# Transitions of a two-layer cross-attention kernel reordered: first loads and K/V, end of the attention, seam to layer 1

## The reference

```python
# layer 0: 32 query heads of 32, 8 key/value heads (4 query heads share one)
q = x @ Wq + bq;  k = ctx @ Wk + bk;  v = ctx @ Wv + bv
attn = softmax(q k^T / sqrt(32) + mask)            # over 64 keys
x = layer_norm(attn v @ Wo + bo + x) * gamma + beta
# layer 1: 16 heads of 64, no biases
a = layer_norm(ctx) * ln_gamma + ln_beta
Q = x @ Wq1.T;  K = a @ Wk1.T;  V = a @ Wv1.T
attn = softmax(where(mask, Q K^T / 8, -inf))
out = x + tanh(gate) * (attn V @ Wo1.T)
```

## Time and profile before

| | |
|---|---|
| median of three runs | 1812.03 us (1809.41 to 1812.71) |
| profiled execution, its own time | 1808.57 us |
| its span | 1806.8 us |
| PE busy | 1737.9 us, 96% |
| DVE, ACT, POOL busy | 60%, 32%, 61% |
| mean granted clock of TensorE | 0.99 |
| DMA | 278 MB, 154 GB/s |

### The profile page before, as it was taken

One profiled execution on the slowest core, in us unless ns is written; L12 is line 12 of the kernel. 1 busy time (PEld: TensorE's weight loads), 2 busy tenths in 40 slices (PEclk: granted clock), 3 DMA queues, 4 the chain that ended last, 5 costly groups with the idle time before them and its releaser, 6 DMA issues.

```text
span 1806.8 us, 22550 instructions
## 1 busy us (share of the span) xinstructions
PE 1737.9 (96%) x8576; PEld 1445.9 (80%) x8576; DVE 1090.4 (60%) x1070; ACT 582.8 (32%) x666; POOL 1104.6 (61%) x610
## 2 busy tenths in 40 slices
PE   5999999999999899999999988899999999999998
PEld 4788888888888688888888867788888888888887
DVE  6888888888879444444444453646644664466442
ACT  3444444444445433333333322213311331133110
POOL 3577777777789856565655585536543664466431
PEclk9999999999999899999999989899999999999999
DMA  9433332332326556666667844454845474556332
GB/s 215 107 80 76 85 79 73 88 80 72 75 80 175 171 184 236 207 240 212 233 227 233 291 138 141 140 171 132 256 130 173 130 224 147 163 161 189 124 121 94
DMA packets 273515, 278.02 MB, mean 154 GB/s; under 512 B 64512, under 2 KB 224384, under 8 KB 273408
## 3 DMA queue, kind: packets, MB, share of 16 engines
q1 hardware_dynamic: 272256, 275.53, 49.3%
q10 hardware_dynamic: 1152, 1.05, 0.3%
HBM read 174.77 MB, written 101.71 MB: 153 GB/s over the span
## 4 chain that ended last, share of the span: by engine, by line
PE 64%; DVE 16%; issue 8%; ACT 5%; POOL 3%; DMA 2%; SPq 1%; DVEq 0%; ACTq 0%
PE ps L53 20%; PE ps L55 20%; PE ps L54 20%; DVE small L1023 4%; DVE pr L1046 4%; ACT pr L795 3%; DVE pT0r L1057 2%; DVE pT1r L1057 2%; DVE xT0r L953 2%; ACT ot L789 2%; DVE xT1r L953 2%; PE ps L657 1%; PE ps L665 1%; PE ps L632 1%; POOL oc1l L1276 1%
## 5 line engine op out<-in xcount | busy, mean ns | idle before, releaser
L1324 POOL TENSOR_TENSOR x2Tl<-x2r,x2Th 128x1024 fp32r<-128x1024 f32 x32 | 76.9, 2403 | 292.1 <-ACT x2Th L896 292.1
L1130 DVE STREAM_TRANSPOSE x2r<-xd 128x1024 f32<-128x1024 f32 x32 | 68.7, 2147 | 207.9 <-PE ps L55 207.9
L1264 POOL TENSOR_TENSOR pr<-pr,small 128x1024 f32<-128x1024 f32 x64 | 121.9, 1905 | 99.8 <-DVE small L1052 99.8
L896 ACT CAST x2Th<-x2r 128x1024 fp32r<-128x1024 f32 x32 | 33.7, 1052 | 375.9 <-DVE x2r L1130 375.9
L1259 POOL TENSOR_TENSOR pr<-pr,small 128x1024 f32<-128x1024 f32 x64 | 123.9, 1936 | 20.9 <-DVE small L1027 20.9
L1023 DVE TENSOR_REDUCE small<-pr 128x16 f32<-128x1024 f32 x64 | 78.1, 1220 | 78.2 <-ACT pr L795 78.2
L1281 POOL TENSOR_TENSOR xb<-xb,bo 128x1024 f32<-128x1024 f32 x32 | 78.6, 2455 | 73.6 <-DMA xb<-in_x_dram 73.6
L1295 POOL TENSOR_TENSOR y<-y,bet 128x1024 f32<-128x1024 f32 x32 | 76.8, 2399 | 74.8 <-DVE y L1069 74.8
L1100 DVE TENSOR_TENSOR y<-ps,xb 128x512 f32<-128x512 f32 x64 | 44.0, 688 | 114.1 <-PE ps L55 111.2
L53 PE MATMUL ps<-wo0h,oc0l 128*128 128x512 f32 x256 | 104.4, 408 | 5.5 <-DVE wo0l L977 3.0
L53 PE MATMUL ps<-wo0h,oc1l 128*128 128x512 f32 x256 | 103.1, 403 | 5.7 <-DVE y L1100 5.7
(11 more groups left out here) (368 smaller groups left out, 5503.3 us busy)
## 6 DMA issues: line engine op xcount, KB each, us to landing
o_scratch<-ot SPq DMA_DIRECT2D x256, 64.0 KB, 1.8
ocr<-o_scratch SPq DMA_DIRECT2D x16, 1024.0 KB, 7.4
xb<-in_x_dram SPq DMA_DIRECT2D x32, 512.0 KB, 6.7
x_scratch<-y SPq DMA_DIRECT2D x32, 512.0 KB, 5.2
a_scratch<-ost SPq DMA_DIRECT2D x64, 256.0 KB, 3.5
b_scratch<-ost SPq DMA_DIRECT2D x64, 256.0 KB, 5.0
xd<-x_scratch SPq DMA_DIRECT2D x128, 128.0 KB, 2.9
raw<-b_scratch SPq DMA_DIRECT2D x64, 256.0 KB, 5.9
```

Of the source, the lines that this page charges most:

```text
L1264: nc.gpsimd.tensor_tensor(heads(v), heads(v), mx.unsqueeze(2).to_broadcast([P, TPB * GRP, KEYS]), ALU.subtract)\
L1324: nc.gpsimd.tensor_tensor(x2T[1][:], x2r[:], f32(x2T[0][:]), ALU.subtract).then_inc(x2_lo, 1)
```

## The change

The order of steps is changed at the three transitions, and a few waits and places in memory with it.

- **First loads and K/V.** Wk is requested by ACT ahead of x0 and x1, no longer by SP behind ctx. The biases of q and k come as rows, by three short loads right behind ctx, and PE turns them into columns, for which it waits ahead of ctx's turn; ACT copies them out. DVE makes wk0l before ctxTl, then turns all four x tiles; V's low half goes to POOL; DVE makes the low halves of x tiles 2 and 3, POOL those of 0 and 1. V is computed in PSUM banks of its own and needn't wait for K's evacuation. SP loads K for units 0 and 1 when K's stores are done, then stores V, loads the third piece of Wq, and only then V of units 0 and 1. The loads of gamma1 and beta1 move into slot 11.
- **End of the attention.** Chunk 0 of the output product is loaded in slot 16 and split in quarters in slots 20, 24, 28 and 32, no longer in slots 58 to 62. Wo's groups 5 and 6 are split in slot 63, group 7 in slot 64 ahead of DVE's turn. The statistics of the context's norm come after the queries' low half; its coefficients come behind the first residual; its rows are scaled on ACT in slot 65; chunk 1's low halves are made in slot h = 2.
- **Seam to layer 1.** From chunk 2 on `coefficients` stands between the two halves of `chunk_lo`. The A pieces are loaded two in each of four slots, and DVE makes six of the low halves (0, 1, 2, 4, 5, 7), POOL two (3, 6). The first probabilities have their own place `pd0`, are summed and scaled ahead of the slot's output work, and are loaded right behind their store; B's pieces 2 and 4 to 7 are requested after they are turned. `prob_hi`, `prob_lo` and `turn_prob` of unit 0 move ahead of the B pieces.
- **Last outputs.** PE waits for each half of O by itself, and the last tile is stored in two halves.

```diff
+        pd0 = at("pd0", 140, [P, TPB, D // TPB])
...
+        def a0_low(h):
+            i = h - (LEAD + TAB * KT + 2)
+            return ((0,), (1, 2), (4,), (5,), (7,))[i] if 0 <= i < 5 else ()
...
-            return (6, 7) if u == UNITS else (u - (UNITS - 6),) if UNITS - 6 <= u < UNITS else ()
+            return (7,) if u == UNITS else (5, 6) if u == UNITS - 1 else (u - (UNITS - 6),) if UNITS - 6 <= u < UNITS else ()
+
+        def chunk0(u):
+            i, r = divmod(u - 2 * KT - 4, 4)
+            return i if 0 <= i < 4 and r == 0 else None
...
-            sp.dma_start(wkr[:], w["Wk0"].rearrange("(k p) n -> p k n", p=P)).then_inc(kv_ld0, 16)
+            sp.dma_start(brow[:KT], w["bq0"].rearrange("(g p) -> g p", p=P)).then_inc(b_ld, 16)
+            sp.dma_start(brow[KT:], w["bk0"].rearrange("(h p) -> h p", p=P)).then_inc(b_ld, 16)
+            sp.dma_start(bv_row[:], row(w["bv0"], KV0)).then_inc(b_ld, 16)
...
-            for u in range(2):
-                load_k(u)
-                load_v(u)
...
+            sp.wait_ge(zeroed, 4)
+            sp.wait_ge(kv_st, 16 * 8)
+            load_k(0)
+            load_k(1)
+            store_v()
             load_wq(2)
+            sp.wait_ge(vv_st, 16 * 4)
+            load_v(0)
+            load_v(1)
             load_wq(3)
...
+                if u == KT + 3:
+                    load_norm()
+                if u == 2 * KT:
+                    load_chunk(0)
...
-                    sp.wait_ge(x_turned, NTILE)
-                    load_chunk(0)
...
-                    sp.dma_start(pd[32 * a:32 * (a + 1)], d["p"][u % 2, :, 256 * a:256 * (a + 1)]
+                    sp.dma_start((pd if u else pd0)[32 * a:32 * (a + 1)], d["p"][u % 2, :, 256 * a:256 * (a + 1)]
...
-                    for c in range(4):
-                        load_a0(c)
-                if h == LEAD + TAB * KT + 1:
-                    for c in range(4, KT):
+                if 0 <= (i := h - (LEAD + TAB * KT)) < 4:
...
                     sp.wait_ge(o_done, SLOTS - 4)
-                    for c in range(3):
+                    for c in range(2):
                         load_raw(1, 0, c)
                 if h == SLOTS - 2:
                     load_xd(2)
                 if h == SLOTS - 1:
                     turn_prob(0)
+                    load_pd(0)
 
...
                     sp.wait_ge(o_done, SLOTS)
-                    for c in range(3, KT):
+                    load_raw(1, 0, 3)
+                    sp.wait_ge(p1_turned, 1)
+                    for c in (2, 4, 5, 6, 7):
                         load_raw(1, 0, c)
-                    load_pd(0)
                     for v in range(2):
                         load_xt(v)
...
+            pe.wait_ge(b_ld, 48)
+            nc.tensor.transpose(PJ[0][:, :KT + 2], brow[:], ident[:KT + 2, :KT + 2]).then_inc(b_turned, 1)
...
-                pe.wait_ge(kfull, r + 1)
                 for k in range(KT):
-                    last = three(nc, V[r][:, :KV0], [ctxT[x][:, k, P * r:P * (r + 1)] for x in (0, 1)],
+                    last = three(nc, PJ[r], [ctxT[x][:, k, P * r:P * (r + 1)] for x in (0, 1)],
...
-                after(pe, out_done, 2 * u)
                 for c in range(KT):
                     n, q = divmod(c, 4)
+                    if q == 0:
+                        after(pe, out_done, 2 * u - 1 + n)
...
+            act.dma_start(wkr[:], w["Wk0"].rearrange("(k p) n -> p k n", p=P)).then_inc(kv_ld0, 16)
             load_x(act, 0)
             load_x(act, 1)
+            act.wait_ge(b_turned, 1)
+            nc.scalar.copy(small[:, :KT + 2], PJ[0][:, :KT + 2]).then_inc(b_done, 1)
+            act.wait_ge(kv_ld0, 16)
+            nc.scalar.copy(wk[0][:], wkr[:]).then_inc(kv_hi, 1)
             act.wait_ge(ctx_t, 1)
             for i in range(4):
                 nc.scalar.copy(ctxT[0][:, 2 * i:2 * i + 2, :], C2[:, HALF * i:HALF * (i + 1)]).then_inc(ctx_hi, 1)
-            act.wait_ge(kv_ld0, 16)
-            nc.scalar.copy(wk[0][:], wkr[:]).then_inc(kv_hi, 1)
-            split_x(0)
-            split_x(1)
             act.wait_ge(kv_ld1, 16)
             nc.scalar.copy(wv[0][:], wvr[:]).then_inc(kv_hi, 1)
-            split_x(2)
+            for n in range(4):
+                split_x(n)
+            split_wq(0)
...
-                if UNITS - 6 <= u < UNITS - 2:
-                    chunk_hi(0, u - (UNITS - 6), 2)
-                if u == UNITS:
-                    for g in wo_groups(u):
-                        split_wo(g)
+                if (i := chunk0(u)) is not None:
+                    chunk_hi(0, i, 2)
+                if u == UNITS + 1:
                     norm_rows(0)
                     norm_rows(1)
...
                     split_x2(v + 1)
-                    exponential(v)
+                if v == 0:
+                    exponential(0)
                 slot(u)
                 if u >= UNITS:
                     out_slot(u - UNITS)
                     prepare(u - UNITS)
+            for c in range(2):
+                split_ab(1, 0, c)
+            exponential(1)
             affine(NTILE - 1)
-            for c in range(5):
-                split_ab(1, 0, c)
             prob_hi(0)
-            for c in range(5, KT):
+            for c in range(2, KT):
                 split_ab(1, 0, c)
             for u in range(2, NTILE):
...
+            dve.wait_ge(kv_hi, 1)
+            nc.vector.tensor_tensor(wk[1][:], wkr[:], f32(wk[0][:]), ALU.subtract).then_inc(kv_lo, 1)
             for i in range(4):
                 split_ctx(ctxT, i, i + 1)
-            turn_x(0)
-            turn_x(1)
-            dve.wait_ge(kv_hi, 1)
-            nc.vector.tensor_tensor(wk[1][:], wkr[:], f32(wk[0][:]), ALU.subtract).then_inc(kv_lo, 1)
-            turn_x(2)
-            turn_x(3)
-            dve.wait_ge(kv_hi, 2)
-            nc.vector.tensor_tensor(wv[1][:], wvr[:], f32(wv[0][:]), ALU.subtract).then_inc(kv_lo, 1)
-            dve.wait_ge(b_ld, 48)
+            for n in range(4):
+                turn_x(n)
+            dve.wait_ge(b_done, 1)
             for h in range(2):
                 dve.wait_ge(k_done, h + 1)
                 nc.vector.tensor_scalar(kf[:, h], V[h][:, :CTX], bk[:, h:h + 1], SCALE0, ALU.add, ALU.mult).then_inc(kfull, 1)
+            split_x(2)
+            split_x(3)
+            split_wq(0)
...
-                if u in (UNITS - 2, UNITS - 1):
-                    norm_stats(2 * (u - (UNITS - 2)))
-                    norm_stats(2 * (u - (UNITS - 2)) + 1)
...
+                if u == UNITS:
+                    split_wo(7)
...
-                if u == 0:
-                    dve.wait_ge(y_done, SLOTS)
...
-                if 0 <= (i := h - (LEAD + TAB * KT + 2)) < 4:
-                    low(0, 0, 2 * i + 1)
+                for c in a0_low(h):
+                    low(0, 0, c)
...
                     mask_max(v)
+                if v == 0:
+                    total(0)
                 slot(u)
                 if u >= UNITS:
                     out_slot(u - UNITS)
                     prepare(u - UNITS)
-                if v >= 0:
-                    total(v)
+            turn_prob(0)
+            total(1)
             gamma(NTILE - 1)
-            turn_prob(0)
             for c in range(1, KT, 2):
                 low(1, 0, c)
...
-            for n in range(4):
+            pool.wait_ge(kv_hi, 2)
+            pool.wait_ge(kv_lo, 1)
+            nc.gpsimd.tensor_tensor(wv[1][:], wvr[:], f32(wv[0][:]), ALU.subtract).then_inc(kv_lo, 1)
+            for n in range(2):
...
-                if UNITS - 5 <= u < UNITS - 1:
-                    chunk_lo(0, u - (UNITS - 5), 2)
-                if u == UNITS:
-                    norm_coefficients()
+                if (i := chunk0(u)) is not None:
+                    chunk_lo(0, i, 2)
...
                     residual(0)
+                    norm_coefficients()
                 if half == 1 and n + 1 < NTILE:
                     residual(n + 1)
+                if h == 2:
+                    for i in range(2):
+                        chunk_lo(1, i)
...
-                if h % 4 == 1 and h // 4 + 1 < NCHUNK:
-                    for i in range(2):
-                        chunk_lo(h // 4 + 1, i)
+                later = h % 4 == 1 and 1 < h // 4 + 1 < NCHUNK
+                if later:
+                    chunk_lo(h // 4 + 1, 0)
                 if half == 1:
                     coefficients(n)
+                if later:
+                    chunk_lo(h // 4 + 1, 1)
...
-                if 0 <= (i := h - (LEAD + TAB * KT + 2)) < 4:
-                    low(0, 0, 2 * i)
+                if h == LEAD + TAB * KT + 3:
+                    low(0, 0, 3)
+                if h == LEAD + TAB * KT + 6:
+                    low(0, 0, 6)
...
                     center(v)
+                if v == 0:
+                    scale(0)
                 slot(u)
                 if u >= UNITS:
                     out_slot(u - UNITS)
                     prepare(u - UNITS)
```

(9 more changed lines are left out.)

84 lines of the change are left out of this document (47 added, 37 removed).

## The result

| | before | changed |
|---|---|---|
| median of 5 runs | 1810.8 us | 1801.9 us |
| lowest to highest | 1809.4 to 1812.7 | 1800.3 to 1803.7 |
| ratio, 95% interval | 1 | 0.9953 (0.9942 to 0.9964) |
| profiled execution, its span | 1808.6, 1806.8 | 1800.3, 1798.5 |

A forecast was written before the change was run, and what follows sets the result against it. PE, busy 96% of the span, was taken as the bound, so only its idle and slow time could be won; -3.6 + 4.6 - 0.3 - 9.9 - 8.0 - 2.0 = -19.2 against 1812.0 gave 1793 us, range 1779 to 1804.

The forecast's parts named there:

- Start, -3.6: First loads and K/V: first scores and first sum 3.1 us earlier, 0.5 more from Wq's third piece; 3.6 us gained.
- The 4.0 us for kb: nothing: At the start, PE's 4.0 us wait for unit 2's kb load was priced at no gain, as DVE sets those scores.
- Rival (c): At the start, bias loads hold ctx's turn to 13.6: gain 1, not 3.6, 1796 us; chance counted in the forecast's 0.60.
- Chunk 0 in the middle, +4.6: Units 20, 24, 28, 32: an added ACT cast (0.5) and POOL subtraction (0.6) lengthen the chain; 4.6 us lost in all.
- taking them away gives nothing by itself: End of the attention: removing chunk 0's eight instructions from their old place gains nothing, since the chain had slack there.
- End of the attention, -0.3: Last units to half tile 3: waits are exchanged, new ones of 5 for pT0l and 4 for ctxn; 0.3 us gained.
- Seam, first part, -9.9: PE's 8.2 us waits for y and two clock falls, 12.0 us lost, shrink to 2.1 of waiting; 9.9 us gained.
- 2.1 of waiting left: Seam, first part: waiting that remains after going through slots 54 to 60 in series, 2.1 us.
- Seam, second part, -8.0: Wait for probT0l and its clock fall, 11.6 us, go, less 3.6 of new waits; 8.0 us gained.
- 3.6 of new waits: Seam, second part: 3.6 us from raw loads held until the turn and POOL's work within 20 us.
- Rival (a): Seam moves its waits: DVE's A pieces cost +5, POOL's queue before output 0 costs +4; 1802 us, chance 0.17.
- End, -2.0: Last outputs: 1.5 us from PE needing only half of O, 0.5 from halving the last store; 2.0 us gained.

The follow-up runs named there:

- the start alone: The kernel before with only the change's edits to the first loads and K/V: 1806.2 us, ratio 0.9975.
- all of the second part relieved: Changed kernel with B4's low half on DVE, POOL's order, B5 to B7's places, raw 2 and 7, and xd of tile 3 altered: 1792.5 us, ratio 0.9896.
- all that gained: Changed kernel with chunk 0 back at the end, norm turns later, residual's load first, second part relieved, kb of unit 2 earlier: 1780.2 us, ratio 0.9829.

## Why the prediction was half right

- **Start, -3.6.** The size is near, by luck in part. One trace shows 5.3 and the start alone measured 4.5. The path forecast, K's stores, then the loads of K at 41 and the first scores 3.1 earlier, wasn't what bound: the loads were requested at 37.48, 6.8 earlier than before and 3.5 ahead of the forecast, and the first scores came 4.4 earlier, behind PE's own chain from K. That K's 5.7 shrank to 4.4 came mostly from POOL's xT0l (1.97 of waiting), not from DVE's work ahead of K's low halves. "The 4.0 us for kb: nothing" was wrong in part of the executions, where kb costs 1 to 3 us. Rival (c) had PE's turn of ctx at 13.6; it began at 12.5, and at 11.7 to 12.9 in the other kernels with this order. With the bias rows behind it, it began at 11.8, so they cost 0.7 to 0.8 at most; the rest of the loss against 10.5 is the context itself, which lands later, although the prediction took it that Wk takes from ctx no more than x0 and x1 did.
- **Chunk 0 in the middle, +4.6.** Right: 4.1, with ACT's cast at 0.5 and POOL's share at 0.5 for 0.6 (these two terms make 4.4; the sum took 1.15 a part). The sign named for it fell short: from 205 to 342 us PE's waits for qs0l grew by 1.1 and those for pT0l by 1.4, not by 4 to 5 together; the lead shows the cost, the list of waits only part of it. That "taking them away gives nothing by itself" was right too: put back at the end, they cost nothing there.
- **End of the attention, -0.3.** Right, by the steps named: waits of 2.8 for pT0l and 4.9 for ctxn (5 and 4 forecast), pT0l at 604.0 and half tile 3 at 620.54, which with the lead of 1.1 are 605.2 and 621.7 in the old times (605 and 622.4 forecast). Two smaller steps came short and did no harm, since pT0l sets the pace: S(63) gained 0.7 of the 1.9, and the wait for wo0l, forecast to go, is 1.7 of 3.0. I took PE's order as given and did not see that the wait for ctxn could be hidden behind half tile 2.
- **Seam, first part, -9.9: the step that failed is "2.1 of waiting left".** It was made by going through POOL's and DVE's instructions in series and took every load as landed. The residual's load was not: POOL idled 3.05 us for it, PE's wait was 4.3 ("below 3" was the sign named), and behind it the clock fell again (0.50 over 4 us), so 4.9 came. Of the missing 5.0 the order of the loads explains 2.3 (the residual's load put first, in one trace against one). In that kernel the wait is still 2.7 with long forms on POOL beside DVE's pieces, 0.6 over the 2.1, and the clock falls behind it too (0.59), which accounts for the 1.9 that are left. I had charged the fall from 3 us of idling on, yet had charged it to the old wait of 2.56 as well, behind which the clock was at 0.65: the sum used two rules.
- **Seam, second part, -8.0: the step that failed is "3.6 of new waits".** They were 4.9 and 3.5, 8.4 in all, each with a slow stretch behind it. I had counted POOL's instructions "within 20 us" as a sum, not in their order against the piece that PE needs third; and I had not read the wait of B5 to B7 for the last store of y, which put the store's landing, 4.8 us, into the chain. The held raw loads, which I named, cost about 1 us. Taking away both causes and the held loads together gave 7.7 on before (all of the second part relieved), which shows that they are the cause, though not the share of each. Rival (a), "the seam moves its waits", with 1802, is nearest to what happened: +5 in the first part came as 5.0, but by the residual's load and the clock, not by DVE's pieces alone, and +4 for POOL's queue as 8.5. That its 1802 fits the time so well is partly luck, since the start gave more than forecast.
- **End, -2.0.** 1.3 came. The waits for xt (1.9) are gone and one of 1.6 for probT1l of the last tile is new; how much the halved store gave was not separated.
- The 0.9 us within the folded weights were not forecast, and their cause stays open.

I had written that I would be wrong if PE still waited over 5 us for y or probT0l. It waited for neither, and the time was missed all the same: the test named the waits that were to go, and not those that could replace them.

## What to carry to other kernels

When a wait is removed, write down for each of the next operands the bottleneck engine needs, one by one, when it is ready in the helper's own order, with its loads and with every semaphore that its first writer waits for; a sum of busy time over the window hides the third operand in the row. A buffer that reuses the space of another stage waits for that stage's last store, so lay it over what is free first. And before a single trace is taken for the size of a part, compare the traces of other kernels that leave this part alone. And independent work of the bottleneck engine itself (here half tile 2) is the cheapest cover: moving two turns by one place gave about as much as the largest part of the change (5.1 us by the leads and 5.8 by the times; the start 5.3 and 4.5).

## What the runs showed of the hardware that was not expected

- A wait under 3 us can be enough for a slow stretch behind it. From 590 us on, over all 14 traces, every wait of 2.9 us or more was followed by a granted clock of 0.50 to 0.66 over the next 4 us, and every one between 1.2 and 1.8 us by 1.00. Between 2.0 and 2.9 us it went either way: 0.57 behind a wait of 2.06 (for probT1l of the last tile, in the kernel with y of tile 31 and B2l ahead of the scaling), and two values behind the same wait of 2.8 for pT0l, in the kernel with the turns one place later (first row) and in the one with all that gained (second row):

```profile
604.65:608.65 4.00, 4.00 (x11) 3.15 (x12) 2.12 (x3) 0.88 (x1) 4.00 (x2) 0.57 0.00 0
598.73:602.73 4.00, 4.00 (x18) 3.31 (x19) 2.12 (x3) 0.88 (x1) 4.00 (x2) 1.00 0.00 0
1046.87:1050.87 4.00, 4.00 (x13) 3.17 (x14) 3.97 (x4) 0.00 (x0) 4.00 (x2) 0.68 0.32 131
```

- The first matmul behind a wait doesn't tell whether the clock falls. The third row, again with all that gained, stands behind a wait of 2.67 for y: its first matmul took 0.47 us, and yet the clock was 0.68 over 4 us and 0.89 over the next 4. So read the granted clock of the stretch.
- Three of the four small instructions of `coefficients` on POOL (128x1) take 0.19 us elsewhere and the third 0.55. The first two took 1.17 and 1.18 where DVE was splitting A1 (until 1036.98) and then A2 (until 1038.11) beside them, and each ended with DVE's instruction:

```profile
1035.85 1.17 POOL L1319 TENSOR_TENSOR small<-small 128x1 f32<-128x1 f32 x1
1036.98 1.18 POOL L1320 TENSOR_TENSOR small<-small 128x1 f32<-128x1 f32 x1
```

- Stretches with the same instructions differ from one execution to the next: by 3.8 us in the first 80 us (the leads from 2.5 to 6.3), by 0.1 from there to unit 62, by about 1 at the end of the attention, and by some 2 us in each of the seam's parts. There part of it is the clock behind a wait of the same length (0.60 and 0.50 behind 5.7 us in the two traces with the old first part).
